# Attention of a language-model tower: the next group's front chain spread over other slots of the turn

## The reference

```python
h = base_weight[x] + lora_A.T[x] @ lora_B.T             # token embedding plus a rank-16 part
a = layernorm(h)                                        # per token, width 512
cq  = layernorm(a @ W_dq)  * q_ln_g  + q_ln_b           # width 128
ckv = layernorm(a @ W_dkv) * kv_ln_g + kv_ln_b          # width 128
Q, (K, V) = cq @ W_uq, split(ckv @ W_ukv)               # 16 heads of 32
h = h + softmax(causal(Q K.T / sqrt(32))) V @ W_o.T     # attention within a sequence
h = h + ffn(layernorm(h))                               # shared part plus 16 routed experts, top 8
```

## Time and profile before

| | us |
|---|---|
| median of 3 runs | 2832.59 (2831.61 to 2834.22) |
| span of the profiled execution | 2827.3 |
| the execution's own time beside its span | not listed apart; the span is 5.3 below the median |
| one regular turn of attention | 68.3 |
| end of attention in the trace, about | 1154 |

### The profile page before, as it was taken

One profiled execution on the slowest core, in us unless ns is written; L12 is line 12 of the kernel. 1 busy time (PEld: TensorE's weight loads), 2 busy tenths in 40 slices (PEclk: granted clock), 3 DMA queues, 4 the chain that ended last, 5 costly groups with the idle time before them and its releaser, 6 DMA issues.

```text
span 2827.3 us, 48754 instructions
## 1 busy us (share of the span) xinstructions
PE 2587.2 (92%) x13025; PEld 1862.0 (66%) x13120; DVE 1841.2 (65%) x3742; ACT 1816.8 (64%) x4597; POOL 1199.2 (42%) x1275
## 2 busy tenths in 40 slices
PE   4899999999999999689999999999999999999999
PEld 2566566666666665467767777777776776777776
DVE  5666666666666665486676576576567667657665
ACT  2666666666666667375675575576567567567566
POOL 3333333333333333044464464454445446446345
PEclk9999999999999999799999999999999999999999
DMA  3011212211111111332122212212212212221221
GB/s 104 24 61 60 60 62 66 66 64 60 60 60 60 63 45 67 106 112 98 53 82 79 81 50 86 80 44 90 83 38 97 82 49 86 79 73 58 86 67 57
DMA packets 99807, 197.67 MB, mean 70 GB/s; under 512 B 10928, under 2 KB 10928, under 8 KB 99568
## 3 DMA queue, kind: packets, MB, share of 16 engines
q1 hardware_dynamic: 94576, 179.29, 18.9%
q0 software_dynamic: 5120, 17.31, 2.6%
HBM read 128.89 MB, written 34.08 MB: 58 GB/s over the span
## 4 chain that ended last, share of the span: by engine, by line
issue 28%; POOL 26%; DVE 2%; PE 2%; DMA 1%; ACT 1%; POOLq 0%; SPq 0%; DVEq 0%
POOL t_lo L1111 24%; POOL sh_lo L1111 1%; DVE t L1478 0%; POOLq L1109 0%; DVE t L1471 0%; DVE f_lo L1495 0%; DMA x<-h 0%; PE ps_y L1126 0%; DMA w_rows<-wT 0%; PE fwork L1126 0%; PE fwork L1128 0%; ACT x L1270 0%; PE fwork L1127 0%; PE ps_y L1128 0%; DMA fres<-in_w_ffn 0%
## 5 line engine op out<-in xcount | busy, mean ns | idle before, releaser
L1111 POOL TENSOR_TENSOR t_lo<-t,t_hi 128x512 fp32r<-128x512 f32 x512 | 738.1, 1452 | 483.8 <-ACT t_hi L1325 483.4
L1471 DVE TENSOR_TENSOR t<-ps_u,square 128x512 f32<-128x512 f32 x544 | 372.5, 685 | 318.5 <-PE ps_u L1128 123.4
L377 POOL TENSOR_TENSOR probs<-probs,inv 128x512 f32<-128x512 f32 x256 | 265.0, 1040 | 626.1 <-DVE inv L774 625.8
L1478 DVE TENSOR_TENSOR t<-t,w_all 128x512 f32<-128x512 f32 x512 | 505.6, 987 | 34.8 <-DMA w_all<-w_rows 6.2
L599 ACT ACTIVATE probs<-ps_s,nmax 128x128 f32<-128x128 f32 x1024 | 362.5, 370 | 221.2 <-DVE nmax L769 221.1
L1325 ACT ACTIVATE t_hi<-t 128x512 fp32r<-128x512 f32 x512 | 320.6, 626 | 263.4 <-DVE t L1478 261.8
L1308 ACT ACTIVATE square<-ps_g 128x512 f32<-128x512 f32 x544 | 316.3, 581 | 91.2 <-PE ps_g L1128 89.1
L1312 ACT ACTIVATE square<-square 128x512 f32<-128x512 f32 x544 | 344.1, 632 | 17.3
L488 PE MATMUL ps_s<-k_diag,qT 128*128 128x512 f32 x512 | 262.3, 594 | 7.8 <-DVE qT L745 1.1
L1126 PE MATMUL ps_y<-t_hi,f_hi 128*128 128x512 f32 x512 | 227.7, 445 | 39.9 <-POOL t_lo L1111 38.9
L1126 PE MATMUL ps_u<-xl_hi,f_hi 128*128 128x512 f32 x512 | 213.6, 417 | 46.4 <-DVE t L1471 46.4
(11 more groups left out here) (195 smaller groups left out, 5446.4 us busy)
## 6 DMA issues: line engine op xcount, KB each, us to landing
w_all<-w_rows SPq DMA_DIRECT2D x256, 256.0 KB, 3.1
res_next<-h SPq DMA_DIRECT2D x64, 256.0 KB, 2.3
res<-res_next SPq DMA_DIRECT2D x64, 256.0 KB, 2.3
h<-res SPq DMA_DIRECT2D x64, 256.0 KB, 2.0
x<-h SPq DMA_DIRECT2D x16, 1024.0 KB, 6.1
fres<-h SPq DMA_DIRECT2D x16, 1024.0 KB, 7.4
out<-fres SPq DMA_DIRECT2D x64, 256.0 KB, 3.1
fres<-in_w_ffn SPq DMA_DIRECT2D x14, 512.0 KB, 3.6
```

Source lines behind the costliest of these rows:

```text
L377: pool.tensor_tensor(probs[:, s % 4, :, :], probs[:, s % 4, :, :], inv[:, s % 4, :].rearrange("p (h o) -> p h o", o=1).to_broadcast([P, HP ...
L1111: pool.tensor_tensor(lo, t[:, j % 2, :], hi.bitcast(F32), ALU.subtract).then_inc(t_lo_done, 1)
L1471: dve.tensor_tensor(t[:, j % 2, :], ps_u[:, j % 2, :], square[:, j % 2, :], ALU.mult).then_inc(t1_done, 1)
L1478: dve.tensor_tensor(t[:, j % 2, :], t[:, j % 2, :], w_all[:, e % 2, :], ALU.mult).then_inc(t_done, 1)
```

## The change

It moves table entries and four of the step constants, swaps two reads in DVE's order, and moves `split_ar` from step 0 of the turn that uses it to step 12 of the turn before (`SPLIT_AT`), where it splits group n + 2. The first split stands ahead of the turns. Since turn 14 does not split any more, DVE's loop is one turn shorter and that turn is written out.

```diff
-MIDWAY = {1: (("art", 1), ("h", 0), ("h", 1)), 2: (("h", 2), ("v", 0)), 3: (("h", 3), ("q", 2)),
-          4: (("v", 2),), 5: (("v", 3),), 7: (("out", 0), ("xt", 3)), 8: (("out", 1),),
-          9: (("out", 2),), 14: (("k", 0),)}
-END = {0: (("k", 1), ("art", 0)), 1: (("q", 1),), 2: (("v", 1),), 3: (("k", 2),),
-       5: (("xt", 0), ("xt", 1)), 6: (("xt", 2),), 7: (("wd", 0), ("wd", 1)),
-       9: (("q", 3), ("k", 3)), 10: (("out", 3),), 11: (("ct", 0), ("ct", 1)), 15: (("q", 0),)}
+MIDWAY = {0: (("art", 0), ("art", 1)), 1: (("h", 1),), 2: (("v", 0), ("h", 3)), 3: (("q", 2),),
+          4: (("v", 2),), 5: (("v", 3),), 6: (("xt", 0), ("xt", 1)), 7: (("out", 1),),
+          9: (("out", 2),), 10: (("k", 3),), 14: (("k", 0),)}
+END = {0: (("k", 1), ("h", 0)), 1: (("q", 1), ("h", 2)), 2: (("v", 1),), 3: (("k", 2),),
+       5: (("out", 0),), 6: (("xt", 2), ("xt", 3)), 7: (("wd", 0),), 8: (("wd", 1),),
+       9: (("q", 3),), 10: (("out", 3),), 12: (("ct", 0), ("ct", 1)), 15: (("q", 0),)}
 FRONT = ("art", "h", "xt", "wd", "ct")
 
-STATS_AT, NORM_AT, C_NORM_AT = (2, 3), 5, 10
+STATS_AT, NORM_AT, C_NORM_AT, SPLIT_AT = (1, 2), 4, 11, 12
...
-GATHER_AT, RSTD_AT, C_RSTD_AT = 5, 4, 9
+GATHER_AT, RSTD_AT, C_RSTD_AT = 4, 3, 10
...
                         row_max(n, step)
+                    read_work(n, END.get(step - 1, ()), LATER)
                     read_work(n, MIDWAY.get(step, ()), SOON + LATER)
-                    read_work(n, END.get(step - 1, ()), LATER)
...
                     if ahead:
-                        if step == 0:
-                            split_ar(n + 1)
+                        if step == SPLIT_AT and not is_turn(n, GROUPS - 2):
+                            split_ar(n + 2)
...
             dve.wait_ge(loaded, 16)
+            split_ar(0)
             turn(-1)
             turn(0)
-            with dve.Fori(1, GROUPS - 1) as n:
+            with dve.Fori(1, GROUPS - 2) as n:
                 turn(n)
-            turn(GROUPS - 1)
-            turn(GROUPS)
+            for n in range(GROUPS - 2, GROUPS + 1):
+                turn(n)
```

## The result

The changed kernel takes **3002.9 us** (median of 4 runs, 2971.9 to 3020.9) against 2832.8 for the kernel before (2831.6 to 2834.2): 1.056 times as long, 95% interval 1.053 to 1.059. The forecast was slower with a chance of 0.90 and 2919 us in a range of 2868 to 2957; the time lies 46 us above the upper end. (The longest of the four runs is left out of the ratio as disturbed.)

What follows compares the result with a forecast made beforehand. TensorE's instruction order was taken to bound a turn: new waits of +9.9 us minus 4.7 removed gave +5.2 a turn, +76 us in all. With +10 for the clock, 2832.6 became 2919 us, range 2868 to 2957.

Steps and rivals of the forecast that it cites:

- k1: TensorE's wait at product k1 for ScalarE's copy of `art` 0, behind slot 0's exponentials: +2.75 us a turn.
- k0: TensorE's wait at product k0 in slot 14 until both halves of c are split: +2.4 us a turn.
- `xt` 1: Transposes `xt` 1 wait for output product 0's bank, summed on VectorE after slot 6's maximum: +1.05 us a turn.
- v1: Product v1 waits for v0's bank, drained by ScalarE behind the exponentials of slot 2: +1.1 us a turn.
- `xt` 2: Transposes `xt` 2 wait until `xt` 0 is drained by ScalarE's copy and VectorE's subtraction: +0.7 us a turn.
- `art` 1: `art` 1 at step 0 waits for q0's bank, drained by VectorE's copy: +0.5 us a turn.
- h1: Product h1 waits for k1's bank, drained by VectorE's three copies: +0.7 us a turn.
- Failed step 1: `ct` 0 at the end of step 12 waits for c normalised on VectorE in step 11: +0.7 us a turn.
- Failed step 2: The first split, ahead of the turns, is the same 1.2 us in another place: 0.
- a feed-forward part that changes by more than a few us: One of the signs named beforehand that would show the prediction wrong; no size beyond a few us.
- The clock: Half clock after the new pauses at k1 and k0, in under half of the turns: 0.7 a turn, +10 us.
- rival (1): Clock falls in every turn at k1 and k0: 24 to 48 us in place of 10, 2933 to 2957; chance 0.2.

Runs made afterwards that it cites:

- experiment 5: experiment 2 with ScalarE copying `art` 0 ahead of the exponentials of slot 0 in step 0: 2906.0 us, one execution.
- 4: experiment 2 with `wd`, Newton steps, `c_norm` and `ct` back in their old steps: 2897.4 us, one execution.
- experiment 1: The kernel before with 143 idle VectorE instructions, its feed-forward code that much further on: 2875.8 us, ratio 1.014.
- experiment 2: The changed kernel with 113 idle VectorE instructions, its feed-forward loop 256 further on than in the kernel before: 2946.0 us, ratio 1.044.
- experiment 7: The kernel before with only the split of `ar` moved to step 13 of the turn before, code aligned: 2857.4 us, ratio 1.008.
- experiment 9: experiment 7 with the mask matmul of slot 1 issued five times in place of once: 2834.4 us, ratio 0.9998.
- experiment 6: experiment 2 with VectorE making `o_lo` 0 ahead of `c_norm` in step 11: 2960.0 us, one execution.
- experiment 10: experiment 7 with ScalarE copying its part of k1 ahead of the exponentials of slot 0: 2836.6 us, ratio 0.9999.

## Why the prediction was right and wrong

**Right: the sign and the mechanism.** TensorE's order, two banks and in-order drains predicted seven waits, each within 0.3 us: k1 2.7 (2.75 forecast), k0 2.5 (2.4), `xt` 1 1.0 (1.05), v1 0.8 (1.1), `xt` 2 0.7 (0.7), `art` 1 0.7 (0.5), h1 0.6 (0.7). The cause of the largest is shown by experiment 5 (+2.6 a turn), that of the c half by 4 (+3.4). The 2.5 of k0 is in part luck: two steps of its chain had other sizes and cancel. The subtraction for `ar` took 0.23 us and not 1.08, and the one for `c_lo` 2.11 and not 1.28 (see the last section). Two sums were off without effect: k1's copy ends at S+3.78 by its own terms, which gives 2.7, and the lower bound by its own terms is +2.9 a turn and not +3.3.

**Failed step 1: "`ct` 0 at the end of step 12 needs c normalised in step 11", +0.7.** I asked when c is ready and who reads it, but not what is queued behind `c_norm` on VectorE. That is `o_lo` 0, then the bank of slot 8's values: 1.6 us, and it swallows the 0.7. The waits then come to 10.6 a turn and not 9.9. TensorE's busy time is up by 0.8 (64.03 against 63.24), where I had "its work itself does not change"; no run shows why. Together this makes +6.8 and not +5.2. In the profiled execution the 13 turn lengths sum to 980.9 us against 887.8, +93.1: twelve of +6.8 give 81, and the first, 80.1 us at a mean clock of 0.90, 12. The other 11.5 of the 104.6 are turn 14 and the turns around that have not all parts. I had +76 for all this.

**Failed step 2, the largest: "the first split ahead of the turns is the same 1.2 us in another place: 0", and no term at all for the feed-forward part.** I priced the instructions that were written out as work and not as code. They moved VectorE's later loop by 143, and that costs 38 us in the profiled execution, 42 (experiment 1) to 57 (experiment 2 against the changed kernel) by medians. The prediction itself names a feed-forward part that changes by more than a few us as a sign that it is wrong. This term alone puts the time outside the range: aligned, the changed schedule takes 2946.0 us, within 2957, though above the 2933 that the forecast itself was given. Nothing in the trace before would have priced it; it should have stood as a risk in the range, since the written-out turn was in the diff.

**The clock: +10 us forecast, the place wrong.** I put it into the regular turns, after the pauses at k1 and k0. In the profiled execution these pauses, 2.7 and 2.5 us, bring no fall: the clock is 1.00 in all twelve turns. In experiment 7 it falls after 1.6 us, and experiment 9 shows the price by filling the pause. The length of one pause thus did not decide; which pattern does, no run here shows. The row that I built on is also weaker than I read it: the clock was at 0.50 from 107.8 us on the earlier trace rows, half a us before the pause of turn 0 ended at 108.32, and not after it. What the profiled execution does pay stands elsewhere: 44 us of attention at half clock against 29, nearly all ahead of the twelve regular turns, and the 60 us more behind attention. Two other executions of the changed kernel, 18 and 44 us above the profiled one, have mean clocks of 0.969 and 0.957 against 0.976. That fits half clock in more turns, my rival (1) in part. The two early turns of experiment 6 show that it can happen with nearly these waits; for the changed kernel's own other executions there is no trace, so it is argued and not shown.

**The sum.** Profiled: 81 in the regular turns, 23 around them, 38 in the feed-forward part, 142.8. The median adds 27 more (170 between the medians). Forecast: 86.

## What to carry to other kernels

When a step is moved on an in-order engine, list what is queued behind it there and who waits for that, not only its own reader. Code written out on one engine shifts all later loops of that engine: pad it back to a place that is known to be good (here 256 instructions further on) before a schedule is judged, or 42 us of fetching are taken for the schedule. A shorter list of waits is no gain until the granted clock has been looked at; where a pause cannot go, repeated matrix work that changes no result can be cheaper than the pause.

## What was not expected of the hardware

- VectorE's instruction fetch: a loop of 274 instructions lost up to 4.1 us in a pass, 8 to 12 times in an execution, each time with a packet of instructions in the pause; at its old place and 256 further on it lost none, 15 or 143 further on it did. Attention, where VectorE's loop has 209 instructions, shows no instruction packet at all from 300 to 1050 us, before or after.
- A clock that falls after 1.6 us of pause (experiment 7) and not after 2.7 and 2.5 (profiled turns of the changed kernel). A fall costs 1.5 us a turn (67.15 against 68.65 in experiment 10).
- Two of VectorE's subtractions take longer when a product of GpSimd runs beside them, in every turn of both traces from 280 to 1080 us; no experiment varied it alone. The subtraction for `ar` takes 1084 ns in the earlier trace rows, with GpSimd's product running from 535.90 to 536.94, and 225 after, where that product ends at 572.77, before the start at 572.85. With `c_lo` it went the other way. There GpSimd's product of 1.40 us starts at 576.53 in the changed kernel, beside it. VectorE's groups by line from 280 to 1080 us in the kernel before (behind the bar the sum in us, then the mean ns of one):

```profile
L738 DVE TENSOR_TENSOR cT_lo<-cT,cT_hi 128x512 fp32r<-128x512 f32 x24 | 15.4, 683 | 0.0
L667 DVE TENSOR_TENSOR ar<-gath,ar 128x64 fp32r<-128x64 f32 x11 | 11.9, 1084 | 0.0
```

and in the changed kernel:

```profile
L738 DVE TENSOR_TENSOR cT_lo<-cT,cT_hi 128x512 fp32r<-128x512 f32 x20 | 21.1, 1094 | 0.0
L667 DVE TENSOR_TENSOR ar<-gath,ar 128x64 fp32r<-128x64 f32 x10 | 2.3, 225 | 0.0
```
